# Softmax attention inside a fused kernel: whole tiles of maxima ahead of each two scores on PE, output copies two exponentials sooner on ACT, POOL's second split ahead of two subtractions

## The reference, cut to what matters

```python
b, l, e = x.shape                      # 2, 1024, 128; H = 16 heads of HD = 8
q = (x @ Wq.T + bq).reshape(b, l, H, HD).transpose(0, 2, 1, 3)
k = (x @ Wk.T + bk).reshape(b, l, H, HD).transpose(0, 2, 1, 3)
v = (x @ Wv.T + bv).reshape(b, l, H, HD).transpose(0, 2, 1, 3)
q, k = _apply_rope(q, cos, sin), _apply_rope(k, cos, sin)
scores = jnp.einsum('bhsd,bhed->bhse', q, k) * (1.0 / np.sqrt(HD))
attn = jax.nn.softmax(scores, axis=-1)
out = jnp.einsum('bhse,bhed->bhsd', attn, v)
return out.transpose(0, 2, 1, 3).reshape(b, l, e) @ Wo.T + bo
```

## Time and profile before

| | |
|---|---|
| time, median of 3 runs | 896.29 us (895.56 to 899.32) |
| span of the profiled execution | 897.0 us |
| PE busy | 730.6 us (81%) |
| DVE busy | 680.8 us (76%) |
| ACT busy | 513.7 us (57%) |
| POOL busy | 244.0 us (27%) |
| mean granted TensorE clock | 0.894 |

### The profile page before, as it was taken

One profiled execution on the slowest core, in us unless ns is written; L12 is line 12 of the kernel. 1 busy time (PEld: TensorE's weight loads), 2 busy tenths in 40 slices (PEclk: granted clock), 3 DMA queues, 4 the chain that ended last, 5 costly groups with the idle time before them and its releaser, 6 DMA issues. The chain is left out here.

```text
span 897.0 us, 18627 instructions
## 1 busy us (share of the span) xinstructions
PE 730.6 (81%) x7062; PEld 355.7 (40%) x7062; DVE 680.8 (76%) x1355; ACT 513.7 (57%) x1012; POOL 244.0 (27%) x297
## 2 busy tenths in 40 slices
PE   6999978887417999928887999999999999945980
PEld 2333246543317999924111222222222222324870
DVE  7868975457884555547786999999999998865655
ACT  3744422565503444453346888888888888922553
POOL 0130010314026777461651200000000100006773
PEclk9999979988757999968658999999999999965995
DMA  3430010000361111132876040404120000022113
GB/s 97 112 78 3 1 25 5 4 3 0 142 258 45 52 48 48 32 105 66 233 158 203 2 85 2 84 3 85 33 53 3 2 2 3 11 103 91 54 49 98
DMA packets 40624, 55.60 MB, mean 62 GB/s; under 512 B 12552, under 2 KB 28048, under 8 KB 39896
## 3 DMA queue, kind: packets, MB, share of 16 engines
q1 hardware_dynamic: 36568, 46.28, 19.3%
q0 software_dynamic: 3968, 8.13, 3.2%
HBM read 35.45 MB, written 14.75 MB: 56 GB/s over the span
## 5 line engine op out<-in xcount | busy, mean ns | idle before, releaser
L1032 DVE TENSOR_REDUCE arena<-psum 128x1 f32<-128x1024 f32 x256 | 301.1, 1217 | 23.2 <-PE psum L916 20.4
L1171 ACT ACTIVATE arena<-psum 128x512 f32<-128x512 f32 x512 | 265.8, 604 | 53.4 <-PE psum L935 53.3
L916 PE MATMUL psum<-arena 56*128 56x512 bf16 x512 | 181.4, 413 | 10.5 <-DVE arena L1032 8.8
L935 PE MATMUL psum<-arena 59*128 59x512 bf16 x512 | 156.4, 390 | 4.8 <-ACT arena L1171 3.6
L946 PE MATMUL psum<-arena 128*32 128x512 f32 x1024 | 138.2, 611 | 8.7 <-issue 8.7
L371 PE MATMUL psum<-arena 128*128 128x128 f32 x808 | 108.1, 281 | 0.4 <-DVE arena L422 0.4
L935 PEld LDWEIGHTS psum<-arena 59*128 59x128 bf16 x512 | 38.3, 94 | 165.8 <-ACT arena L1171 141.8
L371 PEld LDWEIGHTS psum<-arena 128*128 128x128 f32 x808 | 102.1, 198 | 0.7 <-DVE arena L422 0.7
L1240 POOL TENSOR_SCALAR arena<-arena 128x16 f32<-128x16 f32 x16 | 4.1, 254 | 249.4 <-DVE arena L1032 249.2
L487 POOL DMA_INDIRECT rows_y<-arena x62 | 61.6, 993 | 36.7 <-DVE arena L436 29.4
L398 PE MATMUL psum<-arena 128*128 (+1 forms) x496 | 67.1, 279 | 2.0 <-ACT arena L466 1.4
(11 more groups left out here) (317 smaller groups left out, 1071.0 us busy)
## 6 DMA issues: line engine op xcount, KB each, us to landing
arena<-scr_k SPq DMA_DIRECT2D x15, 448.0 KB
arena<-scr_q SPq DMA_DIRECT2D x15, 448.0 KB
arena<-in_f_up SPq DMA_DIRECT2D x1, 4096.0 KB, 12.5
arena<-rows_y SPq DMA_DIRECT2D x12, 256.0 KB, 4.9
scr_q<-arena SPq DMA_DIRECT2D x6, 384.0 KB, 3.9
arena<-in_f_down SPq DMA_DIRECT2D x1, 2048.0 KB, 17.9
rows_x<-xn SPq DMA_DIRECT2D x2, 1024.0 KB, 14.1
arena<-in_f_up SPq DMA_DIRECT2D x1, 2048.0 KB, 9.6
```

The source lines that it names most:

```text
L916: mm = pe.matmul(ps[:, bank + half, :], q[rows, k, h, (qh * 4 + qt) * P:(qh * 4 + qt + 1) * P], kk[rows, k, h, half * BLK:(half + 1) * BLK ...
L935: pe.matmul(ps[:, score_bank(n), :], kk[0:KA, k, h, kb * P:(kb + 1) * P], q[0:KA, k, h, qh * BLK:(qh + 1) * BLK], start=True, stop=True).t ...
L1032: dve.tensor_reduce(mx[:, qh, h * 4 + qt:h * 4 + qt + 1], ps[:, bank:bank + 2, :].rearrange("p a b -> p (a b)"), X, ALU.max).then_inc(S("a ...
L1171: act.activation(pt[:, (u % 3) * HG + h, :], ps[:, score_bank(n), :], ACT.Exp, scale=float(HD) ** -0.5).then_inc(S("a1_exp"), 1)
```

## The change

Three pieces. On PE, the two halves of a tile now stand together and ahead of the two scores that they were woven into. On ACT, the copy of a finished sum stands after the second exponential of its unit and not after the fourth. On POOL, `subtract(n)` is called by hand after each `rotate(n)`, in the same places as before but for block 7, whose subtractions now come after the split of set 1.

```diff
@@ attn1_pe
         for i, n in enumerate(beside or (None, None)):
-            scores(u, 2 * i)
             if n is not None:
                 max_half(n, 0)
+                max_half(n, 1)
+            scores(u, 2 * i)
             scores(u, 2 * i + 1)
-            if n is not None:
-                max_half(n, 1)
             if i == 0 and u >= 2:
                 values(u - 2)
@@ attn1_act
             act.activation(pt[:, (u % 3) * HG + h, :], ps[:, score_bank(n), :], ACT.Exp, scale=float(HD) ** -0.5).then_inc(S("a1_exp"), 1)
+            if h == 1 and u > 1 and u % NTB == 1:
+                act.wait_ge(S("a1_pv"), u - 1)
+                act.copy(o[:, u // NTB - 1, :], ps[:, 7, :]).then_inc(S("a1_o"), 1)
...
-        if u > 1 and u % NTB == 1:
-            act.wait_ge(S("a1_pv"), u - 1)
-            act.copy(o[:, u // NTB - 1, :], ps[:, 7, :]).then_inc(S("a1_o"), 1)
@@ attn1_pool
         pool.wait_ge(S("a1_r0"), n + 1)
-        subtract(n)
...
     rotate(7)
     split_rows(1)
+    subtract(7)
     split_rows(2)
```

More of the change, by code:

```diff
@@ L1252, in attn1_pool @@
     rotate(4)
+    subtract(4)
     pool.wait_ge(S("a1_v"), NB)
@@ L1256, in attn1_pool @@
     rotate(5)
+    subtract(5)
     split_rows(0)
     rotate(6)
+    subtract(6)
     rotate(7)
     split_rows(1)
+    subtract(7)
     split_rows(2)
```

## The result

The changed kernel takes 915.17 us (median of 4 runs, 913.78 to 916.28). Beside it the kernel before took 897.48 us (895.56 to 899.32, 4 runs). The ratio is 1.020, with a 95% interval of 1.0175 to 1.0224: 2.0% slower. The median lies just over the likeliest range of the prediction, 909 to 915. The profiled execution has a span of 912.5 us, forecast 912.2, and is the fastest of the four runs, 913.78 us.

The account below looks back on a forecast made before the run. The prediction took a closed chain through PE and ACT, 2.40 us a unit, as the bound: 897.0 + 24.4 - 9.7 + 0.5 = 912.2 us span, less 0.7 for a median of 911.5; likeliest 909 to 915, wider range 903 to 925.

Parts of the forecast that it names:

- The chain: Loop: exponential, scores h = 1, values pass and next scores h = 2 wait on each other, 2.40 us a unit.
- Part 1: PE's order: both halves ahead delay the scores h = 2 by 0.23 us in 106 units, +24.4 us.
- rival (C): PE's order: halves cost the chain nothing while copies and split are gained, 888.4 us; chance 0.08.
- The row at 482.64: Trace before unit 8: scores started with a half that waited 5.28 us, read as no matmul passing the one ahead.
- rival (A): PE's order: scores do not overlap the second half, coming 0.46 us behind the values pass, 936 us; chance 0.09.
- Rival (B): PE's order: the load of weights is laid bare, 0.09 us a unit, 921 us; chance 0.11.
- (E): PE's order: partial cost, scores 0.1 us late in place of 0.23, 897.7 us; chance 0.05.
- Part 2: ACT's copy: moving it takes a 0.69 us wait off the chain in 14 units, -9.7 us.
- Part 3: POOL's split at the start: stall goes, a DMA wait and slow clock replace it, +0.5 us net.
- the slow pass: Start, behind PE's pause before unit 8: values pass at half clock takes 1.93 us for 1.07, +0.9 us.
- Rival (D): Start: the stall at 482.64 is gained whole because set 1's rows land early, 904.8 us; chance 0.10.

Follow-up runs that it names:

- b_behind: Changed kernel with both halves of tile b behind the scores h = 2 again: 888.48 us, ratio 0.993 to the kernel before.
- one_ahead: Changed kernel with only the second half of tile b back behind the scores h = 2: 887.83 us, ratio 0.990 to the kernel before.
- extra_half: Changed kernel with the second half of each tile b in the loop computed twice: 935.77 us, ratio 1.045 to the kernel before.
- pe_only: Kernel before with only PE's new order: 952.44 us against 927.68, ratio 1.027.
- act_only: Kernel before with only ACT's copy moved behind the second exponential: 921.26 us, ratio 0.993 to the kernel before.
- woven: Changed kernel with PE's order as before, keeping ACT's and POOL's pieces: 919.56 us, ratio 0.992 to the kernel before.
- pool_only: Kernel before with only POOL's split of set 1 put ahead of block 7's subtractions: 926.67 us, ratio 0.999 to the kernel before.

## Why the prediction was right, and where it was off

**The chain.** The four steps of 0.43, 0.65, 0.32 and 1.00 stand in the changed kernel as forecast, the first grown to 0.67. b_behind, one_ahead and extra_half show that what stands between the values pass and the scores h = 2 sets the pitch, and nothing else in the order of the tiles does. DVE, busy 38.15 of 40 us before, was not the bound. Behind a transposition, when it has tiles in stock, its reductions follow 1.11 to 1.13 apart; in ordinary units of the kernel before they start 1.14 and 1.25 apart in turn, so it had 0.1 us a unit to spare.

**Part 1, forecast +24.4, measured +26.2** (pe_only less before). The size of the step was 0.23 and is 0.25. The units are 2.64 and not 2.63.

**The step that the record contradicts is how part 1 comes about.** I had the scores start behind the second half and said that no matmul passes the one ahead. The record of the changed kernel shows scores at 605.21, with the first half and ahead of the second at 605.43. Taken alone this start reads like rival (C), yet the price was paid. ACT comes 0.45 after the last half ahead, in the changed kernel (605.43 to 605.88) and with three halves (614.22 to 614.67), and DVE, which waits for that half itself, comes at the same time (605.85 and 614.63). So what follows program order is when the result is told. It may be that the scores do start late and are only recorded early, and then my step would stand; no run here tells. The row at 482.64 that I argued from holds a different case, since the half ahead there was itself held by a semaphore. Price and sum are the same under both readings, so the forecast of this part didn't need luck. For rival (A) I asked whether scores overlap two halves in a row, and they do: 2.64 and not 2.85. Rival (B), a load of weights laid bare, falls with it, and (C) and (E) with the pitch.

**Part 2, forecast -9.7, measured -9.7** (changed less pe_only). The 0.2 that the old order of PE would take back is there: act_only and woven gain 6.9.

**Part 3, forecast +0.5, measured +0.1.** The stall went and the wait for the DMA came, 4.27 us, with the slow clock behind it. Counted from the first scores of all, unit 8's first scores came 1.34 earlier (forecast 1.1). From them to its scores h = 2 it took 2.75 us for 1.95 before, 0.80 more (forecast 0.9 for the slow pass), and from there to those of unit 9 3.02 for 2.39, of which 0.25 is the longer pitch (forecast 0.2) and 0.38 the clock (forecast 0.5). The last DMA of the rows went out 1.99 us earlier than before, of which 1.55 is the earlier beginning of the loop in this execution, so 0.44 is the change's; 0.43 was forecast. Rival (D), the whole stall gained, falls with pool_only at 0.999.

**The total.** The median is 3.7 us over the forecast of 911.5. 1.8 of that is part 1's size. 1.2 is the reference, whose median is 897.48 with its fourth run and was 896.29 when the forecast was made. Part 3 takes 0.4 off, and about 1.1 stays that no run assigns. One reading was off: every run's time on record lies 1.3 to 1.5 us over its span (913.78 and 912.5 here), so the 897.0 of the kernel before belongs to an execution of some 898.3 us, an estimate, and that the median is 0.7 under the span held for that execution alone. That the span came out 0.3 from the forecast is luck: the loop began 1.55 us early in it, and it is the fastest execution of the four.

## What to carry to other kernels

Find the closed chain of a loop and look at what the instruction behind the longest step is; here the first piece of work issued ahead of it, in other rows of the array, was free, and each further one was paid in full, 0.22 to 0.25 us, though the engine had time to spare; and a busy share of 95% on another engine doesn't make that one the bound. Work from another chain belongs behind the instruction that somebody waits for, or beside it, at most one piece ahead. When a stall is taken away at the start of a stage, look along the queue of DMAs for what is late next: here it ate all of the gain, until the DMAs were moved too.

## What the runs showed of the hardware

Matmuls in different rows of the array are recorded as starting out of program order, and are told of in program order: scores at 605.21, ahead of a half at 605.43 that the program issues first, and ACT at 605.88. The Trainium skill, page TensorE: Matmul & The Clock Gate, Part 3, The mechanism, says that matmuls keep program order in start and in end. For the end, what ACT and DVE wait for agrees, 605.88 and 605.85; for the start the trace's record says otherwise. Whether the scores did run that early or are only recorded so, no run here tells. The ends in the record can't decide it: they are modelled, and by them the scores would end at 605.60, ahead of the half at 605.81.

The other matter is the lot of pe_only, act_only, pool_only and woven: before took 927.68 us in it and 894.65 to 897.48 in the others. This lot ran on another chip than the later ones. By the profiles nothing of it lies in the 106 units; the first scores begin at 473.86 to 477.94 us, for 461.18 in the profile of before, and what follows the scores h = 2 of unit 115 takes 151 to 155 us for 140.5. The cause was not looked into.
